# Attention stage of a two-layer transformer kernel: the row maxima's transfers move from ScalarE's queue to SyncE's

## The chip, the cores and the metric

The kernel runs on one core of a Trainium2 chip. The metric is the device time of one execution in microseconds. TensorE is called PE, VectorE DVE, ScalarE ACT, GpSimd POOL and SyncE SP. SP computes nothing here: it issues DMAs, one after the other, in the order in which its program lists them.

## The reference, cut to what matters

The kernel computes two layers on x of shape (8, 512, 256). The change touches the attention of layer 0 alone: 16 heads of 16 columns, 512 tokens, 8 batches.

```python
xn = _layernorm(x, axis=-1)
qkv = jnp.einsum('bsd,hde->bhse', xn, Wqkv) + bqkv[None, :, None, :]
q, k, v = jnp.split(qkv, 3, axis=-1)
score = jnp.einsum('bhsd,bhtd->bhst', q, k)
score = jnp.where(causal[None, None], score, -jnp.inf)
attn = jax.nn.softmax(score / jnp.sqrt(jnp.asarray(HEAD_DIM, x.dtype)), axis=-1)
y = jnp.einsum('bhst,bhtd->bhsd', attn, v)
...
x = x + y_projected + mixture_of_experts(xn)
...
```

After it come a mixture of experts for layer 0, and for layer 1 a gated scan and a second mixture of experts. None of that is touched.

## The kernel before

`mix_phase` is the attention stage, about the first 450 us of the span. Each engine has a program of its own and semaphores join them; nothing reorders within an engine.

**Groups.** The 8 batches of 16 heads are cut into 32 groups of 4 heads. A group's turn on PE takes 12 steps (3 for each head), a batch 48. In the steps of group g, PE also computes the first score products of group g + 2 (`scores_q`, L922 and L925), from which DVE takes the maximum of each row (`maxima`, L757) and at the end turns the 4 x 4 columns of maxima into rows (`turn_maxima`, L765, tile `max_rows`). So `max_rows` of group g is there at the end of the steps of group g - 2. Then four DMAs of 1 KB each (`load_max`, L547) carry it into row 96 of `q_stack`; PE's second product (`scores_k`, L937 to L941) has 97 rows and so subtracts the maximum, ACT takes the exponential of it (`exps`, L537), POOL masks, and PE multiplies by V (L955). The first `scores_k` of group g waits for the four DMAs of g, and stands at step 9 of group g - 1.

**Stacks.** Q and K of the next batch are made within the current one. Their high and low halves are stored to DRAM (`store_hi`, and in `load_stacks` the low part, L359), and six DMAs of 128 KB fetch them back into `q_stack` and `k_stack` (L375, L376), eight heads at a time. This happens twice in a batch: half 0 is stored near step 11 and PE needs it from step 24; half 1 is stored near step 32 and needed from step 0 of the next batch.

**Queues.** In the kernel before, ACT issues `load_max`, two of the four DMAs in each of steps 0 and 1 of a group (`AT_MAX`), and for groups 0 and 1 all four in a row ahead of its first exponential. SP issues everything else: per batch the load of x two batches ahead (`load_x`), the stores for the experts stage (`store_xT`, `store_xn`, `store_x1`), the stores and loads of the stacks, in batch 0 also a 4 MB fill with zeros (L411), and in batch 7 the weights of the shared expert (`load_shared`, L331 to L340), which ACT splits from step 31 of batch 7 on (`split_shared`, L558).

## Time and profile before

| | us |
| --- | --- |
| median of 3 runs | 1208.96 |
| lowest and highest | 1206.2, 1209.35 |
| span of the profiled execution | 1206.9 |
| of that, attention stage after its start (38 to 440) | 402 |

The page gives no other time for the profiled execution than its span; what lies around it is the difference to the runs, some 2 us.

Busy shares over the whole span: PE 92%, DVE 74%, ACT 56%, POOL 44%. In a timeline row the first number is the start in us from the span's begin, the second the length in us, and the square bracket tells how long the engine sat idle ahead of it and what ended that. A "q" behind an engine (SPq, ACTq) marks its sequencer, which issues DMAs. PEld is PE's weight load, which overlaps the matmuls.

### The profile page before, as it was taken

What the parts mean: (1) busy time and instruction counts of PE and PEld (TensorE: products, weight loads), DVE (VectorE), ACT (ScalarE), POOL (GpSimd) and SP (SyncE); (2) the same over time, 40 slices, a digit from 0 to 9 for tenths busy, and PEclk for the clock granted to TensorE, in tenths of its full rate; (3) what the DMA queues carried; (4) which work ended last, traced back from release to release, by engine and by line L of the source; (5) the groups of instructions that cost most, each with busy time, mean ns of one, the idle gap of its engine ahead of it and who ended that gap; (6) DMA issues with size and microseconds to landing.
All of it is one profiled execution on the core that took longest, in us unless ns stands there. A gap on an engine that the chain in (4) does not pass through costs nothing. (4 is left out here: it accounts for less than half of the span.)

```text
span 1206.9 us, 26712 instructions
## 1 busy us (share of the span) xinstructions
PE 1111.1 (92%) x8873; PEld 745.7 (62%) x8905; DVE 897.4 (74%) x2217; ACT 676.1 (56%) x1463; POOL 529.1 (44%) x743
## 2 busy tenths in 40 slices
PE   4789999999999987998999999996999999999998
PEld 2345555555455546887999888983656646546555
DVE  5778887888888757975766657775876877877876
ACT  2256565555556564565656656664654664664653
POOL 5443434334243235844444444423646547447414
PEclk9689999999999999999999999998999999999999
DMA  5538544354533404665232453452241331331211
GB/s 146 112 67 237 102 80 98 80 111 96 93 81 80 99 19 155 215 179 165 79 127 83 119 163 124 126 149 85 89 141 36 106 126 48 105 102 64 96 45 62
DMA packets 105044, 129.36 MB, mean 107 GB/s; under 512 B 14976, under 2 KB 92736, under 8 KB 103936
## 3 DMA queue, kind: packets, MB, share of 16 engines
q1 hardware_dynamic: 93952, 109.27, 33.8%
q0 software_dynamic: 6912, 18.88, 5.6%
q8 instruction: 46, 0.75, 0.3%
q10 hardware_dynamic: 4096, 0.14, 0.2%
q14 instruction: 38, 0.31, 0.1%
HBM read 84.70 MB, written 43.38 MB: 106 GB/s over the span
## 5 line engine op out<-in xcount | busy, mean ns | idle before, releaser
L537 ACT ACTIVATE p<-bank 128x384 f32<-128x384 f32 (+1 forms) x384 | 191.9, 530 | 186.4 <-PE bank L937 118.8
L757 DVE TENSOR_REDUCE neg_max<-bank 128x1 f16<-128x384 f32 (+3 forms) x352 | 219.7, 640 | 64.7 <-PE bank L925 56.4
L452 POOL TENSOR_SCALAR_AFFINE_SELECT p<-p 128x256 f32<-128x256 f32 x256 | 104.1, 410 | 247.3 <-ACT p L537 246.7
L922 PE MATMUL bank<-k_stack,q_stack 96*128 96x384 f16 (+3 forms) x512 | 133.5, 313 | 20.1 <-DVE neg_max L757 13.1
L1377 POOL DMA_INDIRECT fetched<-xn_dram,token_now x80 | 81.2, 1015 | 42.8 <-POOL token_now L1373 30.6
L937 PE MATMUL bank<-q_stack,k_stack 97*128 97x512 f16 (+1 forms) x256 | 91.5, 362 | 6.0 <-ACT p L537 3.5
L2006 POOL TENSOR_TENSOR up_lo<-up_sq,up_hi 128x512 f16<-128x512 f32 x32 | 43.9, 1399 | 120.7 <-ACT up_hi L2063 120.7
L2017 POOL TENSOR_TENSOR he_lo<-he_sq,he_hi 128x512 f16<-128x512 f32 x64 | 79.9, 1268 | 36.7 <-ACT he_hi L2106 36.6
L1461 ACT ACTIVATE a<-xbank,b 128x256 f32<-128x256 f32 (+1 forms) x126 | 58.6, 468 | 51.2 <-PE xbank L149 47.8
L1549 DVE TENSOR_TENSOR h_lo<-h,h_hi 128x256 f16<-128x256 f32 x159 | 68.4, 433 | 24.4 <-ACT h_hi L1470 23.5
L955 PE MATMUL bank<-p,v_aug 128*32 128x512 f32 (+3 forms) x1024 | 83.5, 445 | 0.8 <-DVE o_rows L737 0.8
L147 PE MATMUL ybank<-l_xT_hi,pack_hi 128*128 128x512 f16 x208 | 78.9, 379 | 4.9 <-DVE up_sq L2220 2.5
L922 PEld LDWEIGHTS bank<-k_stack,q_stack 96*128 96x128 f16 x512 | 45.0, 99 | 59.4 <-DVE neg_max L757 40.9
L1468 ACT ACTIVATE h<-prod 128x256 f32<-128x256 f32 x159 | 64.9, 408 | 26.3 <-DVE prod L1543 21.2
L149 PE MATMUL ybank<-l_xT_hi,pack_lo 128*128 128x512 f16 x208 | 78.8, 379 | 0.0
L148 PE MATMUL ybank<-l_xT_lo,pack_hi 128*128 128x512 f16 x208 | 78.8, 379 | 0.0
L925 PE MATMUL bank<-mask_qk,identb 128*128 128x128 bf16 (+1 forms) x321 | 76.9, 240 | 0.0
L1543 DVE SCALAR_TENSOR_TENSOR prod<-xbank,b,a 128x256 f32<-128x256 f32 (+1 forms) x126 | 58.4, 477 | 24.0 <-ACT a L1461 19.3
L147 PE MATMUL ybank<-pack_hi,up_hi 128*128 128x256 f16 x256 | 69.8, 273 | 0.0
L148 PE MATMUL ybank<-pack_lo,up_hi 128*128 128x256 f16 x256 | 69.8, 273 | 0.0
L149 PE MATMUL ybank<-pack_hi,up_lo 128*128 128x256 f16 x256 | 69.8, 273 | 0.0
L1991 POOL DMA_INDIRECT rows_k<-y_routed_dram,slot x56 | 56.5, 1008 | 27.7 <-issue 15.9
(342 smaller groups left out, 3375.2 us busy)
## 6 DMA issues: line engine op xcount, KB each, us to landing
w_bc<-wT_dram SPq DMA_DIRECT2D x8, 2048.0 KB, 8.0
y_routed_dram<-y SPq DMA_DIRECT2D x37, 256.0 KB
w<-in_w SPq DMA_DIRECT2D x10, 704.0 KB, 6.9
pack<-in_pack SPq DMA_DIRECT2D x12, 342.0 KB, 4.1
xr<-in_x SPq DMA_DIRECT2D x8, 512.0 KB, 7.3
xn_dram<-xn SPq DMA_DIRECT2D x8, 512.0 KB, 3.1
qk_hi_dram<-qk_hi SPq DMA_DIRECT2D x16, 256.0 KB, 2.4
qk_lo_dram<-qk_lo SPq DMA_DIRECT2D x16, 256.0 KB, 2.4
```

The costliest lines, as they stand in the source:

```text
L147: pe.matmul(out, hi_a(c), hi_b(c), start=first and x == 0, stop=False)
L148: pe.matmul(out, hi_a(c), lo_b(c), start=False, stop=False)
L149: mm = pe.matmul(out, lo_a(c), hi_b(c), start=False, stop=last and x == n - 1)
L452: pool.affine_select(out=diagonal, in_=diagonal, pattern=[[0, 2], [1, P]], compare_op=ALU.is_ge, fill=0.0, base=0, channel_multiplier=-1). ...
L537: act.activation(p32[:, s // GH % 2, s % GH, cols], s_bank[n][:, 0:cols.stop - cols.start], ACT.Exp).then_inc(p_exp.sem, 1)
L757: dve.tensor_reduce(neg_max[:, g % 2, 0:GH * TT].rearrange("p (h t) -> p h t", t=TT)[:, heads[0]:heads[-1] + 1, j], a_bank[c % 2][:, 0:len ...
L922: pe.matmul(to[:, at * w:(at + 1) * w], q_stack[0:STK, u, h0 + h, j * P:(j + 1) * P], k_stack[0:STK, u, h0 + h, 0:w], start=at == 0, stop= ...
L925: pe.matmul(diagonal, identb[:, :], mask_qk[:, 0:len(heads), :], start=False, stop=True).then_inc(a_psum.sem, 1)
L937: mm = pe.matmul(to[:, 0:S - n * P], k_stack[0:AUG, u, h, n * P:(n + 1) * P], q_stack[0:AUG, u, h, n * P:S], start=True, stop=True)
L955: mm = pe.matmul(out_bank[VW * h:VW * (h + 1), k * P:S], v_aug[:, b % 2, k, GH * (g % NG) + h, :], p32[:, g % 2, h, P_OFF[k]:P_OFF[k] + S ...
L1377: pool.indirect_dma_start(fetched[:, u, half, :], None, dram["xn"], bass.IndirectOffsetOnAxis(token_now[:, u, half:half + 1], 0)).then_inc ...
L2017: pool.tensor_tensor(he_lo[:, e, :], he_sq[:, e % EB, :], he_hi[:, e, :], ALU.subtract).then_inc(he_lo_s.sem, 1)
```

## The change

SP issues the maxima's DMAs. `load_max` moves from ACT's program to SP's and issues all four of a group in a row, behind a wait for `max_rows`. The store of the low half becomes a function of its own, `store_lo`, so that `load_max` can stand between it and the loads of the stacks. In each batch SP's list has a `load_max` at four places: behind `load_x`, between the store and the loads of half 0, behind the loads of half 0, and between the store and the loads of half 1. In the last batch `load_shared` stands behind the last `load_max`.

```diff
-AT_MAX = {0: (0, 1), 1: (2, 3)}
@@ SP's program
-            def load_stacks(b, half):
-
-                u, heads = b % 2, slice(half * NH // 2, (half + 1) * NH // 2)
+            def load_max(g):
+
+                b, h0 = g // NG, GH * (g % NG)
+                sp.wait_ge(max_rows_s.sem, max_rows_s.at(g))
+                for q in range(4):
+                    to = q_stack[STK:AUG, b % 2, h0:h0 + GH, :].rearrange("o h (t q c) -> o q h t c", t=TT, q=4)[:, q]
+                    of = max_rows[32 * q:32 * q + GH * TT, g % 2, :]
+                    sp.dma_start(to.rearrange("o h t c -> o (h t) c"), of).then_inc(max_loaded[g % 2].sem, 16)
+
+            def store_lo(b, half):
                 lo_rows = dram["qk_lo"].rearrange("(a m p) s -> p m a s", a=2, p=P)[:, half]
                 lo_tile = qk_lo[:, :, :].rearrange("p (a m) s -> p m a s", a=2)[:, half]
                 sp.wait_ge(q_lo_s.sem, q_lo_s.at(b, half + 1))
                 sp.wait_ge(k_lo_s.sem, k_lo_s.at(b, half + 1))
                 sp.dma_start(lo_rows, lo_tile).then_inc(qk_stored.sem, 16)
+
+            def load_stacks(b, half):
+
+                u, heads = b % 2, slice(half * NH // 2, (half + 1) * NH // 2)
                 sp.wait_ge(qk_stored.sem, qk_stored.at(2 * b + half))
@@
             load_x(1)
             for half in range(2):
                 store_hi(0, half)
+                store_lo(0, half)
                 load_stacks(0, half)
                 if half == 0:
                     store_xT(0)
             store_xn(1)
+            load_max(0)
             for b in range(NB):
                 if b + 2 < NB:
                     load_x(b + 2)
+                load_max(NG * b + 1)
                 if b + 1 < NB:
                     store_xT(b + 1)
                     store_hi(b + 1, 0)
+                    store_lo(b + 1, 0)
+                load_max(NG * b + 2)
                 if b + 1 < NB:
                     load_stacks(b + 1, 0)
+                load_max(NG * b + 3)
                 if b + 1 == NB:
                     sp.wait_ge(xT_stored.sem, xT_stored.at(0))
                     load_shared()
@@
                     store_xn(b + 2)
                 if b + 1 < NB:
                     store_hi(b + 1, 1)
+                    store_lo(b + 1, 1)
+                    load_max(NG * b + 4)
                     load_stacks(b + 1, 1)
                 if b == 0:
                     tail = dram["y_routed"][...]
@@ ACT's program
-            def load_max(g, quarters):
...
             router_exp(0)
-            for g in range(LEAD):
-                load_max(g, range(4))
             for n in range(U):
                 exps(0, n)
@@
                     if s + 1 < NB * NH:
                         exps(s + 1, n)
-                    if at % (U * GH) in AT_MAX and LEAD < group(s) <= GROUPS:
-                        load_max(group(s) - 1, AT_MAX[at % (U * GH)])
```

SP's list in the second half of batch 1, before. The first row stores the normalised x, the next two store Q and K, the last two are the first loads of the stacks:

```order
L319 DMA xn_dram<-xn 128x4x256 [waits xn_ready]
L350 DMA qk_hi_dram<-qk_hi 128x2x512 [waits qk_hi_s]
L359 DMA qk_lo_dram<-qk_lo 128x2x512 [waits k_lo_s,q_lo_s]
L375 DMA q_stack<-qk_hi_dram 16x8x512 [waits s_psum,qk_stored]
L376 DMA k_stack<-qk_hi_dram 16x8x512
```

The same place after:

```order
L318 DMA xn_dram<-xn 128x4x256 [waits xn_ready]
L349 DMA qk_hi_dram<-qk_hi 128x2x512 [waits qk_hi_s]
L365 DMA qk_lo_dram<-qk_lo 128x2x512 [waits k_lo_s,q_lo_s]
L358 DMA q_stack<-max_rows 1x16x32 [waits max_rows_s]
L358 DMA q_stack<-max_rows 1x16x32 x3
L385 DMA q_stack<-qk_hi_dram 16x8x512 [waits s_psum,qk_stored]
L386 DMA k_stack<-qk_hi_dram 16x8x512
```

A wait for DVE's maxima and four issues now stand between the store and the loads that PE needs next.

SP's list at the turn from batch 0 to batch 1, before. L411 is the 4 MB fill, L315 loads the x of a later batch, L325 stores the turned x:

```order
L375 DMA q_stack<-qk_lo_dram 16x8x512
L376 DMA k_stack<-qk_hi_dram 16x8x512
L411 DMA y_routed_dram<-zeros_f 4096x1x256
L315 DMA xr<-in_x 128x4x256 [waits xb_ready]
L325 DMA xnT_dram<-xT_hi 128x2x256 [waits xT_lo_s]
```

The same place after:

```order
L386 DMA k_stack<-qk_hi_dram 16x8x512
L429 DMA y_routed_dram<-zeros_f 4096x1x256
L314 DMA xr<-in_x 128x4x256 [waits xb_ready]
L358 DMA q_stack<-max_rows 1x16x32 [waits max_rows_s]
L358 DMA q_stack<-max_rows 1x16x32 x3
L324 DMA xnT_dram<-xT_hi 128x2x256 [waits xT_lo_s]
```

The maxima of group 5 now follow the fill and the load of x on one queue.

SP's list in batch 7, before. L331 to L337 load the shared expert's weights, L340 turned tiles of x:

```order
L376 DMA k_stack<-qk_hi_dram 16x8x512
L331 DMA xr<-in_w 128x704 [waits xn_ready,xb_ready,xT_stored]
L334 DMA xn<-in_w 128x704 [waits xn_stored,xT_psum]
L336 DMA qk_lo<-in_w 128x2x256 [waits qk_stored]
L337 DMA qk_lo<-in_w 96x256
L340 DMA turned<-xnT_dram 128x1024 [waits qk_hi_s]
```

The same place after:

```order
L386 DMA k_stack<-qk_hi_dram 16x8x512
L358 DMA q_stack<-max_rows 1x16x32 [waits max_rows_s]
L358 DMA q_stack<-max_rows 1x16x32 x3
...
L330 DMA xr<-in_w 128x704 [waits xn_ready,xb_ready,xT_stored]
L333 DMA xn<-in_w 128x704 [waits xn_stored,xT_psum]
L335 DMA qk_lo<-in_w 128x2x256 [waits qk_stored]
L336 DMA qk_lo<-in_w 96x256
```

Three waits for maxima (groups 29, 30 and 31) now stand ahead of the weights.

## Rows read from the trace of the kernel before

**Rows 1.** Windows: busy us (count) of PE, PEld, DVE, ACT, POOL, clock, DMA share, GB/s

```profile
38.00:440.00 402.00, 373.41 (x3180) 207.72 (x3208) 326.17 (x853) 228.82 (x480) 138.64 (x281) 0.97 0.47 98
```

**Rows 2.** Waits of PE from 110 to 410: us in total, times, longest

```profile
PE bank L965 <- ACT o_cols L552: 2.3, 6, 0.4
PE bank L940 <- ACT p L537: 1.0, 2, 0.6
```

**Rows 3.** Waits of PE's weight loads in the same stretch

```profile
PEld bank L965 <- ACT o_cols L552: 5.3, 13, 0.7
PEld bank L940 <- ACT p L537: 4.0, 11, 0.9
```

**Rows 4.** Lines L547, L765 and L380: min/median/max ns, first and last start

```profile
L547 ACTq DMA_DIRECT2D q_stack<-max_rows x128: 510/607/1955, 38.4 to 434.7; - x128
L765 DVE STREAM_TRANSPOSE max_rows<-neg_max x32: 176/211/215, 38.1 to 432.6; 128x32 f16<-128x32 f16 x32
L380 SPq DMA_DIRECT2D k_stack<-o_cols x2: 571/612/653, 7.5 to 8.2; - x2
```

**Rows 5.** Timeline at the stage's start: second turn of maxima, first products, first exponentials

```profile
46.36 0.21 DVE L765 STREAM_TRANSPOSE max_rows<-neg_max 128x32 f16<-128x32 f16 x1
46.79 0.93 PE L937 MATMUL bank<-q_stack,k_stack 97*128 97x512 f16 x2 [1.19 <-DMA q_stack<-max_rows]
49.14 1.89 ACT L537 ACTIVATE p<-bank 128x512 f32<-128x512 f32 x4 [23.16 <-issue]
49.79 0.61 PE L937 MATMUL bank<-q_stack,k_stack 97*128 97x512 f16 x1 [1.76 <-ACT p L537]
```

**Rows 6.** Timeline of batch 1, half 0: low store, first load, PE's first use

```profile
116.99 0.36 SPq L359 DMA_DIRECT2D qk_lo_dram<-qk_lo  x1
119.14 0.32 SPq L375 DMA_DIRECT2D q_stack<-qk_hi_dram  x1
127.94 0.23 PEld L922 LDWEIGHTS bank<-k_stack,q_stack 96*128 96x128 f16 x4 [0.38 <-DMA k_stack<-qk_hi_dram]
```

**Rows 7.** Timeline of batch 1, half 1: turn of maxima, first load, first use

```profile
142.53 0.21 DVE L765 STREAM_TRANSPOSE max_rows<-neg_max 128x32 f16<-128x32 f16 x1
143.78 0.32 SPq L375 DMA_DIRECT2D q_stack<-qk_hi_dram  x1
153.29 0.23 PEld L922 LDWEIGHTS bank<-k_stack,q_stack 96*128 96x128 f16 x4 [0.39 <-DMA k_stack<-qk_hi_dram]
```

**Rows 8.** Timeline: the same pair in batch 0 and in batch 6

```profile
91.40 0.21 DVE L765 STREAM_TRANSPOSE max_rows<-neg_max 128x32 f16<-128x32 f16 x1
92.17 0.32 SPq L375 DMA_DIRECT2D q_stack<-qk_hi_dram  x1
...
397.39 0.32 SPq L375 DMA_DIRECT2D q_stack<-qk_hi_dram  x1
...
397.97 0.21 DVE L765 STREAM_TRANSPOSE max_rows<-neg_max 128x32 f16<-128x32 f16 x1
```

**Rows 9.** Behind the fill: x's issue and landing, group 5's landings and first use

```profile
96.33 10.75 SPq L315 DMA_DIRECT2D xr<-in_x  x1
...
DMA to landing us min/median/max: 17.4/17.4/17.4
...
DMA to landing us min/median/max: 4.3/4.6/4.9
...
112.45 0.39 PE L937 MATMUL bank<-q_stack,k_stack 97*128 97x512 f16 x1
```

**Rows 10.** Weights' last landing and first split in batch 7; first x alone

```profile
DMA to landing us min/median/max: 7.5/7.5/7.5
...
438.68 0.79 ACT L558 ACTIVATE shared_in<-xr 128x704 f16<-128x704 f32 x1
...
4.81 0.43 DVE L618 BATCH_NORM_STATS2 stats<-xr 128x6 f32<-128x256 f32 x1 [0.95 <-DMA xr<-in_x]
```

**Rows 11.** Windows, columns as in Rows 1: a stretch at the lower clock

```profile
68.00:72.00 4.00, 3.93 (x23) 1.31 (x24) 0.63 (x2) 1.41 (x5) 1.20 (x3) 0.50 0.90 124
```

More of the change, by code:

```diff
@@ L538, in exps @@
                                ACT.Exp).then_inc(p_exp.sem, 1)
-            def load_max(g, quarters):
-                b, h0 = g // NG, GH * (g % NG)
-                act.wait_ge(max_rows_s.sem, max_rows_s.at(g))
-                for q in quarters:
-                    to = q_stack[STK:AUG, b % 2, h0:h0 + GH, :].rearrange("o h (t q c) -> o q h t c", t=TT, q=4)[:, q]
-                    of = max_rows[32 * q:32 * q + GH * TT, g % 2, :]
-                    act.dma_start(to.rearrange("o h t c -> o (h t) c"), of).then_inc(max_loaded[g % 2].sem, 16)
             def out_copy(g):
```

## The prediction, made before the changed kernel was run

> **What bounds the kernel now.** I read the windows of the attention stage first, then the waits of PE, then the timeline of SP's sequencer, and last the landings of single DMAs. In the 402 us from 38 to 440 PE is busy for 373.4, DVE for 326.2, ACT for 228.8 [rows 1]. PE bounds the stage. Issuing DMAs is not counted as busy, so ACT has 128 times 0.607 us, 77.7 us, on top of its 228.8 [rows 4]: 306 of 402, less than PE and than DVE. So ACT does not bound the mean, and the change is worth only what PE waits for ACT. From 110 to 410 that is 2.3 + 1.0 = 3.3 us by PE's rows [rows 2] and 5.3 + 4.0 = 9.3 us by its weight loads, which partly overlap matmuls [rows 3]. The reader should see next that PE does wait for something else at fixed places: each batch's stacks. PE's first weight load from a new half starts at 127.94 and at 153.29, both ended by the DMA [rows 6, 7]. Half 0 looks like that in all of batches 1 to 6, half 1 in three of seven; in the other four the last load lands 0.5 to 2.0 us before its use. So from the store to the first use PE is tied to a chain of fixed length, 127.94 - 116.99 = 10.95 us in half 0 [rows 6]. SP's list is part of that chain, and it is SP that gets the new work.
>
> **What a group of maxima costs SP.** ACT took 0.607 us for one such issue [rows 4]. SP has issued one similar DMA, from one partition with 16 rows: 0.612 us [rows 4]. With some 0.03 us between issues, four take 2.5 us; the low bound is 1.9, if SP issues them like a stack load (0.47 from start to start, as in the list around these rows), the high bound is 4, since one issue took 1.955 [rows 4]. ACT's removed time is the same, 77.7 us.
>
> **Term 1, the start: a gain.** ACT issues the maxima of groups 0 and 1 ahead of its first exponential, so it waits for the turn at 46.36 and starts exponentials at 49.14, though PE had begun the product at 46.79; PE then stands still for 1.76 us [rows 5]. After, ACT starts as soon as the product ends. Also the first product waited 1.19 us for the maxima's landing [rows 5], slowed by a 512 KB load of x beside it, which SP now issues behind them. Together 1.76 + 1.19 = 2.95, **3.0 us gained**; with only the first, 1.8. Nothing hides this gain: the Q and K stores of the next batch follow PE.
>
> **Term 2, ACT relieved in the steps: a gain.** Bounds 3.3 and 9.3 us [rows 2, 3]. But between a store and its stack's first use the chain sets the time, and what PE gains there it gives back as a longer wait. The chains cover 10.95 + (153.29 - 140.1) = 24 us of a batch of 51, 47% (140.1 is the start of half 1's low store). The other half gives 1.7 to 4.9; I take **2.5 us**, nearer the low end, because the idle time of PE itself is the small one.
>
> **Term 3, half 0 of the stacks: a loss.** Before, SP stored at 116.99, waited for the landing, and issued loads from 119.14 [rows 6]. After, it issues maxima in that gap: 116.99 + 0.4 + 2.5 = 119.9, 0.75 later. The maxima are ready by then. The work that hides the four issues is the store's landing, and it covers 1.75 of 2.5 us. PE waits already, so the rest reaches it: 6 batches x 0.75 = **4.5 us lost** (batch 0's store lands late enough to hide it all). With 1.9 us per group it is 6 x 0.15 = 0.9; with issues of 0.8 each, 6 x 1.4 = 8.
>
> **Term 4, half 1: a loss.** Here SP must also wait for DVE's turn, which comes after the store. In batch 1 the turn starts at 142.53; issues from 142.77 to 145.3; the loads began at 143.78, so they are 1.5 later, and PE's use at 153.29 follows them [rows 7]. The same sum for the others: batch 0 gives 91.40 + 0.24 + 2.5 - 92.17 = 2.0 and batch 6 gives 397.97 + 2.74 - 397.39 = 3.3 [rows 8]; batches 2 to 5 lie at 1.55, 1.6, 0.35 and 1.4. The seven sum to 11.7. Four of them have slack between last landing and first use, 1.3, 0.5, 0.8 and 2.0 us, together 4.6. That leaves **7.1 us lost**; with 1.9 us per group 3.2, with 3.2 us per group 11.
>
> **Term 5, behind the 4 MB fill: a loss, once.** SP's load of x at 96.33 sits in issue for 10.75 us and lands after 17.4, at 113.7 [rows 9]. The maxima of group 5 follow it on SP's queue; ACT's own took 4.3 to 4.9 us in the same time, though the fill was on its way [rows 9]. After, SP is 2.0 us late (term 4), leaves the load of x at 109.1, issues until 111.7, and the maxima land behind x, at 115.7 or a little later; I take 116.2. PE needs them at 112.45 [rows 9], moved by 0.7 of term 4: **3.1 us lost**. If they land 1.9 us after issue, ahead of x, it is 0.4; if 4.9 after, 3.5.
> The Trainium skill, page "DMA: Bandwidth & Descriptors", section "Queues, rings and completion order", says that each DMA engine takes packets in turn from the rows that have work, SP and ACT having one row each, and drains one row in ring order. By that rule a small transfer on ACT's row passes a large one and on SP's row queues behind it; it speaks against the change here. The trace agrees for ACT (4.3 to 4.9 us); no row shows the other side.
>
> **Term 6, the shared expert's weights: a loss, once.** The last turn is at 432.6 [rows 4]; four issues end at 435.4; then come the weights, whose second part landed 7.5 us after issue, with stack loads ahead of it [rows 10]. ACT reaches its split at 438.68 [rows 10] and the program order holds its exponentials behind it, so PE stops soon after. From 436.0 + 7.5 = 443.5 the stall is 4.8. But the queue is empty then: the first x of 512 KB, alone, was in use 4.0 us after issue at 0.8 [rows 10]. 704 KB then need some 5 us from 436, 441.2: **2.5 us lost**, bounds 1.3 and 4.8.
>
> The other `load_max` places cost nothing: SP is idle for 5 to 12 us at the turns behind half 0, and behind `load_x` in later batches the maxima have some 4.7 us to spare before their use. If that cover went, it would cost as term 5 does, in six batches.
>
> **Sum.** -3.0 - 2.5 + 4.5 + 7.1 + 3.1 + 2.5 = +11.7 us. The span of 1206.9 becomes 1218.6. The median of the runs shown is 2.1 above that span, so 1220.7, **1221**.
>
> **The rivals.**
> (a) Faster: ACT is what PE waits for, and the later stack loads don't reach PE, because the six transfers drain more slowly (first lands 3.3 us after issue, last 6.5) than they are issued and a later start is caught up. Then term 1 counts 3.0, term 2 the full 9.3, terms 3 and 4 nothing, 5 and 6 stay: -12.3 + 5.6 = -6.7, 1202. It decides in this direction once terms 3 and 4 together stay under 3 us. Against it: the drain begins with the first issue, so it moves with it.
> (b) No change: SP issues a group in 1.9 us. Terms: -3.0 - 4.7 + 0.9 + 3.2 + 0.4 + 1.3 = -1.9, 1207. For it: SP's stack loads take 0.43; against it: the one-partition DMA took 0.612.
> (c) Much slower: a pause of PE of some 3 us behind the fill or at the split lets its clock fall. In 68 to 72 the granted clock is 0.50 (1.2 of 2.4 GHz) [rows 11], right after PE had idled for 2.4 of 4 us, and it lasted 6.8 us; a product takes 0.61 instead of 0.39 there [rows 5, 9], so one such fall costs 6.8 x (1 - 0.39/0.61) = 2.5 us. Two falls, with terms 3 and 4 toward their high ends (+6), give +23, 1232.
> (d) The change doesn't do what it says, in that the maxima land too late on SP's queue in other groups as well. It would add 1 to 3 us in each of six batches, 1230; the 4.7 us to spare speak against it.
>
> **How the numbers follow.** Forecast (+6 to +18) 0.62, (c) and (d) together 0.17, (b) 0.12, (a) 0.09. About 0.3%, 3.6 us, is what a measurement of this kernel can tell from no change. Faster by more: (a), 0.09. Within: (b) and a little of the forecast's low end, 0.14. Slower by more: 0.77. The range leaves out (a), most of (b) and the far end of (c): 1209 to 1231.
>
> **What would show it.** Right: ACT's first exponential at about 46 to 47; the first stack load of half 1 starting 2.5 us after each turn; PE's weight loads of L922 waiting for the DMA by about 1 to 2 us more; one PE wait of about 3 us for the maxima near 113; the split of the shared weights waiting for its DMA near 440. Wrong: four issues in 1.9 us, landings of the stacks that don't move, or a PE that in the steps between the chains runs clearly faster than 51 us per batch, which would mean ACT was worth more than its waits show.

## The result and the profile after

The changed kernel takes 1224.69 us (median of 4 runs, 1222.73 to 1228.05) against 1208.62: a ratio of 1.0141, with a 95% interval of 1.0115 to 1.0167. It is slower by 16.1 us. Its profiled execution took 1222.79 us with a span of 1221.0, which is 14.1 more than the span before. Forecast were +11.7 on the span and 1221 us.

The loss arises in the attention stage. DVE turns the maxima once per group, so the start of each turn is a clock that both kernels have (L765 before, L770 after). The table shows the turn of a group against the same turn in the trace of before; "end" is the last residual addition of the stage, at 460.08 us before and 476.50 after.

| turn of group | 2 | 3 | 4 | 5 | 6 | 12 | 16 | 24 | 30 | end |
| --- | --- | --- | --- | --- | --- | --- | --- | --- | --- | --- |
| before, us | 63.2 | 78.8 | 91.4 | 102.6 | 116.1 | 193.4 | 244.8 | 347.6 | 420.8 | 460.1 |
| after | -2.6 | -5.3 | -3.3 | -3.3 | +2.8 | +6.7 | +8.1 | +12.2 | +15.1 | +16.4 |
| after, run again (e9) | -1.9 | -4.6 | -2.2 | -2.2 | +3.3 | +6.8 | +8.7 | +12.7 | +17.1 | +17.8 |

So the kernel gains 2 to 3 us at the start, loses 2 between turns 3 and 4 (those of groups 3 and 4), loses 6 between turns 5 and 6, and then loses about 2 us in each batch. The lead of 5.3 us at turn 3 is more than the start's gain: the kernel before has its clock at the lower level for 6.8 us from 66.9 on, the changed one for 3.4 us from 63.9 on. The span has 2.3 us less than the end of the stage; in the changed kernel run again nothing comes back (+17.8 at the end, +18.1 in the span), so I take these 2.3 us for the spread of single executions.

Of the profile after, first the windows, columns as in [rows 1]: the stage, and ten microseconds behind the fill.

```profile
38.00:455.00 417.00, 376.00 (x3181) 212.92 (x3211) 328.52 (x852) 229.00 (x478) 138.87 (x280) 0.96 0.45 92
110.00:120.00 10.00, 6.83 (x31) 3.56 (x32) 3.11 (x9) 3.92 (x8) 1.96 (x3) 0.66 0.34 104
```

Against [rows 1], PE needs 15 us more for nearly the same busy time (376.0 against 373.4), so it waits more. The clock of the second window, 0.66, stood at 1.00 before, with 9.15 us of PE busy there.

The stacks that PE needs first in batch 1 (half 0, made in batch 0) are the place between turns 3 and 4. The kernel before, and then the changed one:

```profile
76.64 0.24 PEld L922 LDWEIGHTS bank<-k_stack,q_stack 96*128 96x128 f16 x4 [0.41 <-DMA k_stack<-qk_hi_dram]
```

```profile
73.66 0.40 PE L927 MATMUL bank<-k_stack,q_stack 96*128 96x128 f16 x4 [2.39 <-DMA k_stack<-qk_hi_dram]
```

Waits of PE and of its weight loads from 110 to 424 come next (us, times, longest), the counterpart of [rows 2] and [rows 3]:

```profile
PE bank L927 <- DMA k_stack<-qk_hi_dram: 13.9, 12, 2.1
PE bank L942 <- DMA q_stack<-max_rows: 3.6, 1, 3.6
PE bank L970 <- ACT o_cols L561: 1.9, 5, 0.4
...
PEld bank L927 <- DMA k_stack<-qk_hi_dram: 18.1, 12, 2.4
```

In the row of before for the same matmul (110 to 440), the stacks' DMA had stopped PE for this much:

```profile
PE bank L922 <- DMA k_stack<-qk_hi_dram: 0.9, 2, 0.8
```

From 0.9 us to 13.9: the stacks are what PE now waits for. ACT's row for `o_cols` hardly moved.

The price of a group on SP (ns min/median/max, first and last start), the counterpart of [rows 4]:

```profile
L358 SPq DMA_DIRECT2D q_stack<-max_rows x128: 502/589/1722, 38.9 to 449.6; - x128
```

SP's sequencer and PE in batch 1, half 0 and then half 1, the counterparts of [rows 6] and [rows 7]:

```profile
119.80 0.36 SPq L365 DMA_DIRECT2D qk_lo_dram<-qk_lo  x1
120.21 2.41 SPq L358 DMA_DIRECT2D q_stack<-max_rows  x4
122.72 0.53 SPq L385 DMA_DIRECT2D q_stack<-qk_hi_dram  x1
131.69 0.40 PE L927 MATMUL bank<-k_stack,q_stack 96*128 96x128 f16 x4 [0.92 <-DMA k_stack<-qk_hi_dram]
...
145.84 0.21 DVE L770 STREAM_TRANSPOSE max_rows<-neg_max 128x32 f16<-128x32 f16 x1
146.08 2.40 SPq L358 DMA_DIRECT2D q_stack<-max_rows  x4
148.58 1.21 SPq L385 DMA_DIRECT2D q_stack<-qk_hi_dram  x1
158.41 0.40 PE L927 MATMUL bank<-k_stack,q_stack 96*128 96x128 f16 x4 [1.86 <-DMA k_stack<-qk_hi_dram]
```

In half 0 the first stack load starts 2.92 us behind the start of the low store, 0.77 later than before (2.15), and PE's first use of the stack comes 8.97 us behind that load (8.80 before). In half 1 the loads begin 2.74 us behind the start of DVE's turn, where they began 1.25 us behind it before. The use follows them at 9.8 us (9.5 before). A later load is a later use. Over batches 0 to 6 the loads of half 1 start later, counted from the turn, by 1.98, 1.49, 1.55, 1.60, 0.34, 1.43 and 3.33 us, together 11.7. Those of half 0 in batches 1 to 6, counted from the low store, start later by 0.76 to 0.78 us, and once, in batch 3, by 1.69, together 5.5.

### The profile page after: what moved, and what is told of

The parts are those of the page before. It is cut to its first block and busy times, and to the rows that moved or that the text cites. A ratio compares the mean times of both kernels' runs of the same rounds, so it can differ in the third digit from the quotient of the medians.

```text
span 1221.0 us, 26712 instructions
## 1 busy us (share of the span) xinstructions
PE 1110.2 (91%) x8873; PEld 748.4 (61%) x8905; DVE 897.7 (74%) x2217; ACT 676.9 (55%) x1463; POOL 531.6 (44%) x743
## 5 line engine op out<-in xcount | busy, mean ns | idle before, releaser
L148 PE MATMUL ybank<-l_xT_hi,pack_lo 128*128 128x512 f16 x208 | 78.8, 379 | 0.0
L147 PE MATMUL ybank<-l_xT_lo,pack_hi 128*128 128x512 f16 x208 | 78.8, 379 | 0.0
```

The costliest lines, as they stand in the source:

```text
L147: pe.matmul(out, hi_a(c), lo_b(c), start=False, stop=False)
L148: mm = pe.matmul(out, lo_a(c), hi_b(c), start=False, stop=last and x == n - 1)
```

## The experiments

The experiments ran on three chips. On one ran e1, e2, e7 and e8, on a second e3, e10, e11 and e12, and on both the kernel before takes 1248 us instead of 1209; on the third, with e4, e5, e6 and e9, it takes 1209. The 40 us arise behind 750 us of the span, which no edit touches. Ratios are therefore each to the kernel before as it ran on the same chip beside the experiment. Turns are compared with the one trace of before; one execution's turns differ from the next one's by some tenths of a us even ahead of the stage (turn 0 lies between -0.5 and +1.3).

| run | before on the same chip, us | median, us | ratio, 95% interval | turn 6 | turn 30 | end |
| --- | --- | --- | --- | --- | --- | --- |
| e1 | 1248.09 | 1245.59 | 0.9981 [0.9962, 1.0001] | -6.0 | -6.0 | -5.8 |
| e10 | 1248.60 | 1242.09 | 0.9958 [0.9936, 0.9980] | -4.5 | -4.0 | -3.3 |
| e11 | 1248.60 | 1241.43 | 0.9961 [0.9936, 0.9985] | -3.1 | -2.8 | -2.8 |
| e8 | 1248.09 | 1249.38 | 1.0007 [0.9990, 1.0023] | -1.0 | -1.7 | +1.1 |
| e7 | 1248.09 | 1256.94 | 1.0066 [1.0042, 1.0091] | -0.4 | +5.4 | +5.9 |
| e12 | 1248.60 | 1298.37 | 1.0418 [1.0371, 1.0465] | +6.3 | +50.1 | +50.2 |
| e4 | 1209.41 | 1208.80 | 0.9997 [0.9981, 1.0013] | +1.1 | +0.7 | +1.6 |
| e6 | 1209.41 | 1225.5 (a single run) | | +0.8 | +17.0 | +18.5 |
| e9 | 1209.41 | 1226.02 | 1.0137 [1.0115, 1.0159] | +3.3 | +17.1 | +17.8 |
| e2 | 1248.09 | 1261.44 | 1.0103 [1.0073, 1.0133] | -1.4 | +9.1 | +12.7 |
| e3 | 1248.60 | 1261.46 | 1.0104 [1.0067, 1.0140] | +5.2 | +16.5 | +16.5 |
| e5 | 1209.41 | 1207.04 | 0.9984 [0.9973, 0.9995] | -3.2 | -3.7 | -1.3 |

**The start alone (e1, and e10 the same again).** From the kernel before:

```diff
             store_xn(1)
+            load_max(0)
             for b in range(NB):
                 if b + 2 < NB:
                     load_x(b + 2)
+                if b == 0:
+                    load_max(1)
@@ ACT's program
-            for g in range(LEAD):
-                load_max(g, range(4))
```

> The kernel before, but SP issues the maxima of groups 0 and 1 alone; ACT keeps the other 30 groups. Theory (ACT's first exponential was held by its own issues and their wait): exponentials start near 46 instead of 49, the stage from there on is 3 us earlier and stays so, 1205.6 against 1208.6. Rival (the lead is given back as a longer wait for the stacks of batch 1, half 0): PE waits some 3 us near 74 and the time is 1208.6.

> The kernel with only groups 0 and 1 issued by SP, a second time, beside the next one. Theory: the stage's lead of 3 us or more at the third turn of maxima stays to its end, and the whole is 3 to 6 us faster than before. Rival (the first run's small gain in total, 0.2%, was all there is, because what the stage wins is given back behind it): 2 us.

The stage ends 5.8 and 3.3 us earlier, and the kernel is faster by 2.5 and 6.5 us; the second interval excludes no change. The timeline of e1 at the start of the stage, to be read against [rows 5]:

```profile
45.80 0.93 PE L947 MATMUL bank<-q_stack,k_stack 97*128 97x512 f16 x2 [0.69 <-DMA q_stack<-max_rows]
46.44 1.90 ACT L549 ACTIVATE p<-bank 128x512 f32<-128x512 f32 x4 [21.36 <-PE bank L947]
47.09 0.61 PE L947 MATMUL bank<-q_stack,k_stack 97*128 97x512 f16 x1
```

ACT starts 2.7 us earlier than at 49.14 and is released by PE, no longer by its own issues; PE's stop of 1.76 us is gone, and the wait for the maxima is 0.69 instead of 1.19. Term 1 is real and stands by itself. This version is faster than the changed kernel, and than the one before by 0.2% (not clear of no change) and 0.4%. Of the turns' gain, 2.4 and 2.0 us stand at turn 2, where the start is over. The rest comes up to turn 4: the kernel before has a stretch of 6.8 us at the lower clock from 66.9 on, which e1 has not, so e1's -6 is not the start alone. The rival that was set for e1 came true in part: PE waits 2.24 us at 72.56 for the stacks of batch 1, half 0. It gives back 0.6 us between turns 3 and 4, and the rest of the lead stays.

**The start, with the maxima ahead of the store of x (e11).** From e1:

```diff
-            store_xn(1)
             load_max(0)
+            store_xn(1)
```

> As the run beside it, but the maxima of group 0 stand ahead of the 512 KB store of x on SP's list, not behind it. Theory (SP's queue is drained in its order): PE's last wait of 0.65 us for them at 46 is gone, 0.5 us faster than the run beside it, below what can be told apart in the total but seen in the turns. Rival (that wait is PE's own end of the products): no difference in the turns.

PE's wait for the first maxima is gone. First e11's timeline:

```profile
46.22 0.95 PE L947 MATMUL bank<-q_stack,k_stack 97*128 97x512 f16 x2
```

and the same place of e10:

```profile
46.74 0.13 PEld L947 LDWEIGHTS bank<-q_stack,k_stack 97*128 97x128 f16 x2 [0.68 <-DMA q_stack<-max_rows]
```

The product starts 0.5 us earlier (0.2 us of that stand at turn 0 already), but in the total the two can't be told apart (0.9961 and 0.9958, run side by side).

**ACT relieved, nobody burdened (e8).** From batch 2 on nobody transfers maxima; row 96 keeps those of groups before, so the subtracted maxima are wrong there. PE's and DVE's waits for them end with batch 1.

```diff
-                    if at % (U * GH) in AT_MAX and LEAD < group(s) <= GROUPS:
+                    if at % (U * GH) in AT_MAX and LEAD < group(s) <= 2 * NG:
@@ DVE's wait ahead of its turn
-                dve.wait_ge(max_loaded[g % 2].sem, max_loaded[g % 2].at(g // 2 - 1))
+                dve.wait_ge(max_loaded[g % 2].sem, max_loaded[g % 2].at(min(g // 2 - 1, NG - 1)))
@@ PE's wait
-                if n == 0 and h % GH == 0:
+                if n == 0 and h % GH == 0 and s // GH < 2 * NG:
```

> The kernel before, without the maxima's DMAs of groups 8 to 31 and without PE's waits for them; the products of batches 2 to 7 take whatever maxima lie in the row, so that the softmax there is shifted by other numbers. It is ACT relieved in three quarters of the stage with SP's list untouched. Theory (PE, the stacks and DVE bound the steps): 1 to 3 us gained, 1206 to 1208. Rival (ACT was what PE waited for): 24 of 30 groups of the 9 us that the weight loads waited, 7 us or more gained, 1201.

Through six batches the turns move from -1.0 to -1.9, less than 1 us, and the total is that of before (behind turn 31 it loses 3.0 us; a stretch at the lower clock near 440 is 6.9 us long there and 3.4 before, which is 1.2 of them). Waits of PE in e8 from 110 to 440:

```profile
PE bank L922 <- DVE neg_max L757: 10.7, 27, 0.6
PE bank L965 <- ACT o_cols L552: 2.9, 7, 0.6
PE bank L937 <- ACT p L537: 0.8, 2, 0.7
...
PE bank L940 <- ACT p L537: 0.2, 1, 0.2
```

and the same waits of before:

```profile
PE bank L922 <- DVE neg_max L757: 7.1, 25, 0.6
PE bank L965 <- ACT o_cols L552: 2.8, 7, 0.6
PE bank L940 <- ACT p L537: 2.5, 5, 0.7
```

PE waits for `p` 1.5 us less (2.5 to 1.0), for `o_cols` as long as ever, and for DVE's maxima 3.6 us more. What ACT's relief frees passes to DVE. The other kernels bear this out: from 110 to 415 PE waits for DVE's maxima 5.0 to 7.0 us where ACT issues them all (before, e1, e7, e10, e11) and 8.6 to 9.4 us where ACT is relieved and nothing stands ahead of the stack loads (e4, e5, e8).

**SP burdened, ACT not relieved (e7).** From the kernel before. SP issues four idle DMAs of 1 KB, into a spare tensor, where the changed kernel issues maxima ahead of the stack loads. ACT keeps the real ones.

```diff
+            def idle_max(g):
+
+                sp.wait_ge(max_rows_s.sem, max_rows_s.at(g))
+                for q in range(4):
+                    to = dram["idle"][4 * g + q:4 * g + q + 1, :].rearrange("o (m c) -> o m c", c=32)
+                    sp.dma_start(to, identb[32 * q:32 * q + GH * TT, 0:32]).then_inc(idle_stored.sem, 16)
@@ load_stacks, behind the low store
+                if b >= 1:
+                    idle_max(NG * (b - 1) + 2 + 2 * half)
                 sp.wait_ge(qk_stored.sem, qk_stored.at(2 * b + half))
```

> The kernel before, with ACT carrying the maxima as ever, but SP waits for the maxima of the same groups and issues four idle DMAs of 1 KB to DRAM at the two places between store and stack loads (56 in all). Their data is used by nothing. Theory (what costs is the place in SP's list, since the stacks behind are late already): the first stack load of a half starts 0.7 and 1.5 us later, PE waits at nearly every stack, some waits let the clock fall, and the time is 12 to 15 us longer, 1221 to 1224. Rival (the maxima themselves land late on SP's queue, the place costs little): at most 2 us, 1209 to 1211.

The stage ends 5.9 us later and the total rises by 8.9: a loss without any of the other edits, but about half of what was expected (12 to 15). SP's list in batch 1 of e7, half 0, and the idle issues over the stage:

```profile
116.99 2.11 SPq L358 DMA_DIRECT2D idle_dram<-identb  x4
119.20 0.37 SPq L385 DMA_DIRECT2D q_stack<-qk_hi_dram  x1
...
L358 SPq DMA_DIRECT2D idle_dram<-identb x56: 302/439/1575, 64.5 to 403.7; - x56
```

A part of the shortfall is in these rows: the idle DMA has a median of 0.439 us where the maxima's has 0.589. The first stack load is 0.45 us later in most of half 0 (not 0.77) and about 1.05 in most of half 1 (not 1.5). The other part is that not every delay reaches the turns. Between turns 6 and 30 lie twelve of the places, half 0 and half 1 of batches 1 to 6. Their delays in e7 sum to 4.1 and 8.1 us; less 3.3 of slack the prediction's own working gives 8.9, and e7 loses 5.8. In batch 2, half 0, PE's first use of the stack is 0.5 us later than before (179.3 for 178.8), yet turns 10 and 12 around it stand both at +0.1. Some of the short delays are thus made up behind their place, which the prediction did not reckon with.

**The idle issues doubled (e12).** From e7:

```diff
-                for q in range(4):
+                for q in range(8):
...
```

> The kernel before with eight idle issues instead of four at each of the two places, ACT carrying the maxima. Four took 2.1 us and cost the stage 5.9 us and the whole 8.2. Theory (the cover, the landing of the store, is used up, so each further issue reaches PE whole): four more of 0.53 us at 6 + 7 places are 27 us on top, or a little more with the clock's falls, 1243 to 1250 where before is 1209. Rival (the transfers' drain catches up a late start): less than 12 us on top.

Expected were 27 us on top of e7 in the stage; at turn 30 they are 44.7, and the total is 50 us over before where 34 to 41 were expected. Waits of PE for the stacks (us, times, longest) in e12, from 30 to 500:

```profile
PE bank L933 <- DMA k_stack<-qk_hi_dram: 39.6, 14, 4.7
```

and in e7, from 30 to 470:

```profile
PE bank L933 <- DMA k_stack<-qk_hi_dram: 9.5, 13, 1.5
```

The window from 40 to 440 of e12 (columns as in [rows 1]):

```profile
40.00:440.00 400.00, 348.27 (x2817) 199.21 (x2819) 291.44 (x760) 203.86 (x423) 123.87 (x247) 0.92 0.43 90
```

and of e7:

```profile
40.00:440.00 400.00, 365.56 (x3124) 205.56 (x3154) 323.65 (x847) 224.79 (x471) 134.82 (x274) 0.97 0.47 97
```

The waits alone are 30 us more, 4.4 of them in batch 0, half 0; the list explains them: the first stack load starts 4.45 (half 0) and mostly 6.7 to 7.2 us (half 1) behind the low store, against 2.15 and some 3.6 before. The rest is an estimate from the clock. A mean of 0.92 between the two levels of 1.2 and 2.4 GHz means 64 of 400 us at the lower one; 0.97 means 24. The 40 us of difference, at the loss of 0.36 us per us that prediction (c) took from 0.61 and 0.39 us per product, are 14 us. Together 44. So a longer SP list costs first its own length, and then the lower clock that comes with PE's longer stops.

**ACT keeps every other group (e4).** From the changed kernel: the two `load_max` that stand between a store and its stack loads go back to ACT.

```diff
-                load_max(NG * b + 2)
@@
-                    load_max(NG * b + 4)
@@ ACT's program, with the former load_max
+                    if at % (U * GH) in AT_MAX and LEAD < group(s) <= GROUPS and group(s) % 2 == 1:
+                        load_max(group(s) - 1, AT_MAX[at % (U * GH)])
```

> The changed kernel, but ACT issues the maxima of the even groups from 2 on, as before; SP keeps group 0 and the odd groups, whose places are idle ones. The lists between store and stack loads are those of the kernel before. Theory (terms 3 and 4 are the even groups): of the changed kernel's loss the start's gain (-3 to -6), the fill's loss (+6) and little else stay; the attention stage ends 0 to 3 us after that of before, so 1 to 3 us over before. Rival (SP's odd groups cost as well, by landing late or by lengthening its list): 6 us or more over before.

Between turns 6 and 30 e4 loses nothing (+1.1 to +0.7), where the changed kernel loses 12.3 (+2.8 to +15.1). The total is 17 us below that of the changed kernel, run beside it as e9, and equals before. Half of the maxima are still on SP. It is these two places in SP's list that cost behind turn 6, and not SP's queue as such. Between turns 3 and 4 e4 loses nothing either. PE's wait behind the fill stays in e4, 2.1 us, and with 3.5 us at the lower clock behind it e4 loses 3.3 between turns 5 and 6; that the total equals before is the start's gain against this loss. The rows are from 30 to 470, the second the stacks':

```profile
PE bank L952 <- DMA q_stack<-max_rows: 2.1, 1, 2.1
...
PEld bank L937 <- DMA k_stack<-qk_hi_dram: 3.1, 7, 0.9
```

**Half 1's maxima behind the stack loads (e6).** From the changed kernel:

```diff
                     store_lo(b + 1, 1)
-                    load_max(NG * b + 4)
                     load_stacks(b + 1, 1)
+                    load_max(NG * b + 4)
```

> The changed kernel, but in half 1 the maxima stand behind the stack loads instead of ahead of them. Theory (SP's queue is drained in its order, so they land behind six loads of 128 KB, 13 us after the low store, while PE needs them some 10.5 us after it): PE waits about 3 us for maxima in each of seven batches, the clock falls more often, 10 us or more over the changed kernel. Rival (small transfers pass the large ones): the stack loads start 1.5 us earlier, no wait for maxima, and 5 us under the changed kernel.

The stage ends at +18.5, beside +17.8 for e9: neither the loss nor the gain that the theories named. It is a single run. Waits of PE in e6 (30 to 470):

```profile
PE bank L942 <- DMA q_stack<-max_rows: 13.2, 8, 2.6
PE bank L927 <- DMA k_stack<-qk_hi_dram: 9.8, 7, 4.1
```

The stack loads of half 1 start as they did before (3.15 us behind the store in batch 1, 3.65 before). Now the maxima, issued behind six loads of 128 KB, arrive late, and PE waits for them in six of the seven batches, 1.1 to 2.6 us; the other two of the eight waits are at the start and behind the fill (1.4 us). The two orders end alike only in the sum: between turns 6 and 30 e6 loses 16.2 us (12.3 and 13.8 in the changed kernel), between turns 3 and 4 4.4 (2.0 and 2.4), and between turns 5 and 6 only 1.2 (6.1 and 5.5).
The Trainium skill, page "DMA: Bandwidth & Descriptors", section "Queues, rings and completion order", says that a queue's row on an engine is drained in ring order, while rows take turns; e6 agrees for SP's own queue, since the first of the four maxima landed within 0.3 us of the last stack load in each of its seven batches. The landings during the fill do not decide it: 4.3 to 4.9 us on ACT's queue [rows 9], 3.6 to 5.3 us on SP's in the changed kernel.

**The changed kernel again (e9),** as the neighbour of e4, e5 and e6:

> The changed kernel as it is, beside the others of this call, since this chip's times differ from those of the first comparison. Theory and rival alike: 14 to 16 us over the kernel before of the same call, the attention stage 16.4 us longer.

1.0137 repeats 1.0141, and the turns repeat within 1.1 us up to group 29 and within 2.0 at the last two.

**The 4 MB fill moved (e2).** From the changed kernel, the fill goes from the end of batch 0's list to batch 7:

```diff
                 load_max(NG * b + 1)
+                if b + 1 == NB:
+                    tail = dram["y_routed"][...]
...
@@
-                if b == 0:
-                    tail = dram["y_routed"][...]
...
```

> The changed kernel, but the 4 MB fill is issued in batch 7, behind the maxima of group 29, where the queue is empty. Theory (the maxima of group 5 queue behind fill and x on SP's queue, and the pause then costs the clock): the 3.6 us wait near 113 is gone, the clock stays at 1.00 there, and 6 us come back, 1218.6 against 1224.7. Rival 1 (only the wait counts, the half clock is made up for): 3.6 us, 1221.1. Rival 2 (the fill costs its time wherever it stands): 1224.7.

Between turns 5 and 6 e2 loses 0.6 us, the changed kernel 6.1. With no fill ahead of it, SP's load of x takes 0.43 us to issue (11.27 in the changed kernel), and the maxima of group 5 land 1.7 to 2.3 us after their issue. Its window behind the place of the fill, against 6.83 us and 0.66 above:

```profile
110.00:120.00 10.00, 8.97 (x80) 4.86 (x73) 8.72 (x30) 7.00 (x15) 3.94 (x8) 1.00 0.28 88
```

From turn 6 to turn 30 it loses 10.5 and has no stretch at the lower clock between 79 and 451; its stack waits there (110 to 440) are as in the changed kernel:

```profile
PE bank L927 <- DMA k_stack<-qk_hi_dram: 14.8, 12, 2.3
```

At the end of the stage 3.6 us come on top, with the fill now in the last batch and 6.8 us at the lower clock from 451.2 on. Moving the fill alone is no cure.

**The shared expert's weights ahead of the last maxima (e3).** From the changed kernel:

```diff
                 load_max(NG * b + 1)
+                if b + 1 == NB:
+                    sp.wait_ge(xT_stored.sem, xT_stored.at(0))
+                    load_shared()
@@
                 load_max(NG * b + 3)
-                if b + 1 == NB:
-                    sp.wait_ge(xT_stored.sem, xT_stored.at(0))
-                    load_shared()
```

> The changed kernel, but the shared expert's weights are loaded in batch 7 behind the maxima of group 29 instead of group 31. Theory as predicted (term 6): 2.5 us come back, 1222.5 if the changed kernel is 1225. As its trace says: ACT waited 0.8 us there, so 1 us or less comes back, 1224 to 1225.

The stage ends at +16.5, as without the edit (+16.4). Between turns 29 and 30, where SP now issues the weights, it loses 2.5 us (+14.1 to +16.5; the changed kernel 1.3 and, run again, 2.5), and from there on nothing (the changed kernel 1.3 and 0.8 more). The 2.5 us need no weights to explain them, since e9 has them too, each time with 3.4 us at the lower clock from 425 or 426 on. So what the weights cost is at most the 0.8 to 1.3 us behind turn 30, which are gone in e3. In the total (1.0104, with an interval that reaches 1.0140) e3 can't be told from the changed kernel.

**ACT's half and both long loads moved (e5).** From e4, with the weights and the fill behind `load_max(NG*b+1)` of batch 7.

```diff
                 load_max(NG * b + 1)
+                if b + 1 == NB:
+                    sp.wait_ge(xT_stored.sem, xT_stored.at(0))
+                    load_shared()
+                if b + 1 == NB:
+                    tail = dram["y_routed"][...]
...
```

Both are gone from their old places.

> As the run with the even groups on ACT, and with the 4 MB fill and the shared expert's weights in batch 7 behind group 29. All named losses are gone. Theory: the attention stage ends 5 to 7 us before that of the kernel before, and the whole is 3 to 7 us faster. Rival (PE is bound by its stacks and DVE, and what is gained at the start is given back): no difference.

1207.04 against 1209.41: faster by 2.4 us, with an interval that excludes no change, where 3 to 7 had been expected; the stage ends 1.3 us early, not 5 to 7. Turns 5 to 30 keep the start's gain (-2.9 to -3.9). Then 2.2 us go between turns 30 and 31, where ACT issues its share during the fill. ACT in e5, batch 7:

```profile
417.32 1.90 ACTq L564 DMA_DIRECT2D q_stack<-max_rows  x2
419.30 2.71 ACTq L564 DMA_DIRECT2D q_stack<-max_rows  x2
422.05 0.98 ACT L554 ACTIVATE p<-bank 128x384 f32<-128x384 f32 x2 [2.29 <-issue]
```

The first pair of issues takes 1.90 us and the second 2.71 instead of some 1.2, and the exponentials wait 2.29 us.

## Why the prediction was right, and where its terms were off

The forecast was 1221, the measurement 1224.7, within the range and on the expected side. The main mechanism, SP's issues ahead of the stack loads, was right. Other terms were off in both directions, and one place was overlooked. The terms, with what each measured:

| term | predicted, us | measured, us | from |
| --- | --- | --- | --- |
| 1, start | -3.0 | -2.6 (run again -1.9) | turn 2 |
| 2, ACT relieved | -2.5 | about -0.9 | e8 |
| 3, half 0 of batch 0 | 0 | +2.0 (+2.4) | turns 3 to 4 |
| 3 and 4, the twelve places of batches 1 to 6 | +10.9 | 12.3 (13.8), with the relief and 2 (3) falls of the clock in it | turns 6 to 30 |
| 5, behind the fill | +3.1 | +5.5 | turns 5 to 6, less e2's 0.6 |
| 6, weights | +2.5 | +1.3 (+0.8), of that 0.80 waited for the DMA in after | behind turn 30 |

The 10.9 are the prediction's 4.5 + 11.7 - 4.6 without batch 0's half 1, to which it gave 2.0 less 1.3 of slack.

**What a group costs SP** was right: 2.40 us for 2.5, by 0.589 for one issue.

**Term 1** was right in its two parts (e1), and it is the only part of the change that is worth having. That -3.3 also stands at turn 5 is luck. The lead had grown to 5.3 us at turn 3 by the stretch at the lower clock, and 2.0 of it went at the next place.

**Term 3 in batch 0** was put at nothing, because the store lands late enough there to hide four issues. They did fit: the first load starts 3.46 us behind the low store, 3.62 before. But PE, ahead by the start's gain and the shorter stretch at the lower clock, stood at 73.66 for 2.39 us, and the clock then fell for 3.5 us. The five traces with SP's four issues at this place (after, e2, e3, e6, e9) have waits of 2.4 to 4.1 us there and lose 2.0 to 4.6 us between turns 3 and 4; e1, e4, e5, e8, e10 and e11, without them, lose 0.6 at most. Neither the issues nor PE's lead alone does it: e7, with four idle issues at this place but no lead, waits 0.32 us and loses nothing, and e1, with the lead but no issue there, waits 2.24 us and loses 0.6. How the loss divides between the two, no run separates.

**Term 2** was too large. What was wrong is the reading of PE's idle time behind ACT as time that would come back. PE's rows put 2.3 + 1.0 us down to ACT [rows 2]. The 2.3, for `o_cols`, do not change when ACT is freed of its issues (e8), and what is saved on `p` PE spends on DVE's maxima, for which it waits 3.6 us more. DVE is busy for 326 of 402 us [rows 1] and had 25 such waits in the trace of before, which the prediction did not quote.

**Terms 3 and 4** were right in mechanism, place and delay: 0.77 us in half 0 for 0.75, and 11.7 us over the seven halves 1 for 11.7. e4 shows that both places together carry the loss, and e7 shows that issue time alone makes one: no transfer of maxima and no relief of ACT is needed. With the measured delays the working gives 5.5 + 9.7 - 3.3 = 11.9 us for the twelve places. Measured are 12.3 with some 0.9 of relief and 2.4 of the clock in them, so about 10.8 (11.0 in e9). So a part of the delays was made up, as in e7, and the clock cost more than that saved. In the changed kernel it fell to its lower level at 159.5 and at 265.3 for 3.4 us each, during or right behind waits of PE for the stacks of 1.86 us (at 158.41, above) and 2.08 us:

```profile
265.71 0.61 PE L927 MATMUL bank<-k_stack,q_stack 96*128 96x128 f16 x4 [2.08 <-DMA k_stack<-qk_hi_dram]
```

Its products take 0.61 us at that clock instead of 0.39, which makes 1.2 us for each fall; this price is an estimate. e2 has waits of the same kind without such a fall, so the fall is not certain at this size.
The Trainium skill, page "DMA: Bandwidth & Descriptors", section "Issuing engines are not separate DMA queues", says that issuing from several engines only saves sequencer time, which is "usually small relative to the DMA itself". Here one issue took 0.589 us where the maxima landed 1.73 us (median) after theirs, so it is smaller than the DMA but not small; and PE did not wait for these landings except behind the fill, while 2.4 us of issue time in a list that PE waits for did cost.

**Term 5** was mis-sized, and its mechanism was right only in part. SP's sequencer, the landing of x, the landings of group 5's maxima and PE behind the fill in the changed kernel, against [rows 9]:

```profile
94.52 11.27 SPq L314 DMA_DIRECT2D xr<-in_x  x1
105.83 3.50 SPq L358 DMA_DIRECT2D q_stack<-max_rows  x4
...
DMA to landing us min/median/max: 17.9/17.9/17.9
...
DMA to landing us min/median/max: 3.6/4.2/5.3
...
113.11 0.61 PE L942 MATMUL bank<-q_stack,k_stack 97*128 97x512 f16 x1 [3.58 <-DMA q_stack<-max_rows]
```

SP left the load of x at 105.8, not 109.1, since it had begun 1.8 us earlier than before, and issued the maxima until 109.3. They landed at 111.1, 111.4, 111.7 and 113.1, three of them ahead of x (112.4), which had been issued first. From issue to landing they took no longer than ACT's in the same place (3.6 to 5.3 us for 4.3 to 4.9). So what made them late was SP's sequencer, held in the issue of x behind the fill, and not a place behind x in the queue, as the prediction had it: ACT had issued these four from 102.9 to 105.6. In e2, without the fill, both the long issue and the wait are gone. PE waited 3.58 us. The prediction took the stall as the whole cost. But the clock was at half from 111.7 on, for 6.8 us (the product in this row takes 0.61), and that is 2.5 us more by rival (c)'s own price: 3.6 + 2.5 = 6.1 us between turns 5 and 6, which is what the turns show (in the table, e2's 0.6 is taken off for batch 0's half 1, which lies there too). e9 agrees: 3.72 us of waiting and 3.4 at the lower clock, and 5.5 lost. Rival (c) was set as an alternative to the forecast, at a chance of its own with (d); one of its two falls, behind the fill, happened within it. The other, at the split of the weights, did not come about, nor did (c)'s higher terms 3 and 4.

**Term 6** was too large. The start of the second weights' load and ACT's split:

```profile
450.87 0.39 SPq L333 DMA_DIRECT2D xn<-in_w  x1
...
DMA to landing us min/median/max: 3.5/3.5/3.5
...
454.39 0.79 ACT L567 ACTIVATE shared_in<-xr 128x704 f16<-128x704 f32 x1 [0.80 <-DMA xn<-in_w]
```

The landing took 3.5 us where some 5 were taken. ACT waited 0.80, under the low bound of 1.3. Behind turn 30 the changed kernel loses 1.3 us (e9 0.8), and e3, with the weights earlier, nothing; but e10, with the weights where they were before, loses 0.7 there too, so the term is hardly clear of the spread between executions.

**The sum,** by stretches of the stage. Up to turn 5 the forecast has -3.0, the trace -3.3. From turn 5 to 6 it has 3.1 + 0.7 = 3.8, the trace 6.1. From turn 6 to 30 it has 10.9 - 2.5 = 8.4, the trace 12.3. Behind turn 30 it has 2.5, the trace 1.3. Together that is 11.7 and 16.4; the span shows 14.1 and the medians 16.1. So the forecast lacks 4.7 us. The smaller relief (1.6) and the clock (2.5 behind the fill and 2.4 at the stacks) account for 6.5, less 1.2 for the weights; the rest, -0.6, is within what two executions differ by. That the forecast came so close owes something to luck, too: the 2 us of batch 0's half 0 are balanced by the kernel before's own longer stretch at the lower clock.

**The rivals.** (a) fell: the drain moves with its first issue (8.97 us for 8.80 from first load to first use). (b) fell with the 2.40 us per group; SP's price of a DMA depends on the DMA, as e7's 0.439 shows, and the one-partition row of before was the right neighbour. (d) did not happen: the only wait for maxima on PE between 110 and 424 is the one behind the fill.

**Open** are the share of the issues in the wait of batch 0's half 0, and why the falls of the clock come in some traces and not in others with like waits.

## What to carry to other kernels

Before moving small DMAs to an idle queue, read that queue's list and not its load: four issues of 0.59 us each, put between a store and the loads that PE waits for, delayed these loads by 0.3 to 3.3 us, and over twelve such places some 11 us of it reached PE. The same four cost nothing measurable where SP had been idle (e4), and 5.5 us where a large transfer's issue held SP ahead of them. Relief of an engine is worth only what is left once the next engine in line has taken it, so look for the second waiter before a gain is booked. Where an edit makes a stop of PE, price it with the slower products that may follow it: here 3.6 us of waiting became 6.1.

## What the hardware showed that I had not expected

- One DMA's issue can hold its sequencer for long behind a large transfer: SP's load of x (512 KB) sat 10.75 us (before) and 11.27 us (after) in issue behind the 4 MB fill, and 0.43 us in e2, where no fill was ahead of it. ACT issued four DMAs in the meantime at 0.51 to 0.81 us each.
- On ACT, three single issues of 1 KB took 1.33 to 1.36 us during the fill in e5, about 0.6 otherwise. That the fill is the cause is not shown: in the kernel before one issue took 1.96 us at 64.0, with no fill under way.
- The issue price depends on the form: a 1 KB DMA into one partition took 0.589 us on SP and 0.607 on ACT, the idle one of the same size out of 16 partitions into DRAM 0.439.
- The cost of issue time is not linear: 2.1 us of idle issues per group cost 5.8 us between turns 6 and 30, twice as many cost 43.9. Slack and the landing of the store hide a part of the first four issues and next to nothing of the next four, and the mean granted clock went from 0.97 to 0.92 with PE's longer waits.
- Two other chips ran the same kernel before in 1248 us instead of 1209. The window from 800 to 1200 us has a clock of 0.95 there (e1) and 0.99 in the trace of before. That is 32 us more at the lower level, which at 0.36 us per us makes some 12 of the 37 us lost in the window; what the others are, and why the chips differ, is not known. The window in e1:

```profile
800.00:1200.00 400.00, 353.79 (x2268) 205.90 (x2266) 272.22 (x685) 196.27 (x371) 184.88 (x176) 0.95 0.25 79
```

and in the kernel before:

```profile
800.00:1200.00 400.00, 378.94 (x2533) 229.01 (x2531) 301.23 (x731) 219.98 (x413) 203.66 (x192) 0.99 0.27 88
```
